# Causal attention: the mask moves from products on TensorE into a VectorE instruction that also takes the maximum

## What is computed

```
qkv = einsum('bse,ehd->bshd', x, qkv_w) + qkv_b
logits = einsum('bqhd,bkhd->bhqk', q, k) / sqrt(64)
logits = where(tril, logits, -0.7 * finfo.max)
probs = softmax(logits, axis=-1)
attn = einsum('bhqk,bkhd->bqhd', probs, v)
return einsum('bqhd,hde->bqe', attn, out_w) + out_b
```

## Time and profile before

| | us |
|---|---|
| median of 3 runs | 1450.72 |
| the profiled execution, its own time | 1447.09 |
| the profiled execution, its span | 1445.4 |
| PE busy in the span | 1402.4 (97%) |
| DVE busy | 1244.4 (86%) |
| ACT busy | 930.1 (64%) |
| POOL busy | 968.8 (67%) |

### The profile page before, as it was taken

One profiled execution on the slowest core, in us unless ns is written; L12 is line 12 of the kernel. 1 busy time (PEld: TensorE's weight loads), 2 busy tenths in 40 slices (PEclk: granted clock), 3 DMA queues, 4 the chain that ended last, 5 costly groups with the idle time before them and its releaser, 6 DMA issues.

```text
span 1445.4 us, 29493 instructions
## 1 busy us (share of the span) xinstructions
PE 1402.4 (97%) x10306; PEld 874.0 (60%) x10306; DVE 1244.4 (86%) x1966; ACT 930.1 (64%) x1862; POOL 968.8 (67%) x756
## 2 busy tenths in 40 slices
PE   8989999999999999999999997989999999999998
PEld 6645555555555555555555554556767676676777
DVE  7578788788887888878888787689999999999997
ACT  3367677766776667767677675657665576657552
POOL 5145555556555556555656554659999999999895
PEclk9999999999999999999999999999999999999999
DMA  8058777868778778787877867300000000000000
GB/s 194 1 120 208 188 172 186 198 163 193 182 175 198 167 188 194 175 193 166 194 187 180 191 163 200 91 0 1 1 8 8 1 8 1 8 9 1 8 1 15
DMA packets 77149, 164.13 MB, mean 114 GB/s; under 512 B 31410, under 2 KB 43724, under 8 KB 77004
## 3 DMA queue, kind: packets, MB, share of 16 engines
q1 hardware_dynamic: 77004, 162.24, 47.1%
HBM read 9.08 MB, written 2.10 MB: 8 GB/s over the span
## 4 chain that ended last, share of the span: by engine, by line
PE 81%; DVE 9%; issue 5%; POOL 3%; ACT 2%; DVEq 0%; POOLq 0%; ACTq 0%
PE accum L1111 17%; PE both L1045 13%; PE both L2805 8%; PE flips_all L1045 6%; PE flips_all L1137 4%; PE flips_all L2828 4%; PE misc L1009 4%; PE flips_all L1009 4%; PE flips_all L2817 3%; PE flips_all L2865 2%; PE flips_all L1022 2%; PE misc L1022 2%; PE accum L2817 2%; PE accum L2828 1%; PE flips_all L2851 1%
## 5 line engine op out<-in xcount | busy, mean ns | idle before, releaser
L462 POOL TENSOR_SCALAR big<-big,recip 128x384 f32<-128x384 f32 (+7 forms) x512 | 374.5, 746 | 401.1 <-DVE recip L714 400.8
L722 DVE STREAM_TRANSPOSE big<-big 128x896 f32<-128x896 f32 (+7 forms) x288 | 345.7, 1223 | 20.1 <-POOL big L462 19.4
L1111 PE MATMUL accum<-across,v_sb 128*64 128x256 f32 (+1 forms) x2560 | 281.9, 363 | 12.6 <-issue 12.5
L543 ACT ACTIVATE big<-both,neg_max 128x1024 f32<-128x1024 f32 (+3 forms) x256 | 242.2, 949 | 45.6 <-DVE neg_max L704 29.8
L704 DVE TENSOR_REDUCE neg_max<-both 128x1 f32<-128x1024 f32 (+3 forms) x256 | 248.5, 1011 | 24.5 <-PE both L1050 21.9
L1111 PEld LDWEIGHTS accum<-across,v_sb 128*64 128x64 f32 x2560 | 178.3, 137 | 138.7 <-issue 71.7
L1045 PE MATMUL both<-qk_sb 64*128 64x512 f32 (+3 forms) x1024 | 213.5, 535 | 10.5 <-ACT big L543 9.8
L543 ACT ACTIVATE big<-flips_all,neg_max 128x256 f32<-128x256 f32 (+3 forms) x256 | 132.0, 524 | 106.2 <-DVE neg_max L704 81.3
L1613 POOL TENSOR_TENSOR prod<-xnT,qs 128x1024 f32<-128x1024 f32 (+3 forms) x32 | 180.3, 5642 | 8.9 <-DVE qs L2318 8.9
L704 DVE TENSOR_REDUCE neg_max<-flips_all 128x2 f32<-128x512 f32 (+3 forms) x128 | 102.2, 819 | 93.8 <-PE flips_all L1050 93.1
L2805 PE MATMUL both<-slow_sb,h_T 128*128 128x512 f32 x384 | 179.7, 594 | 1.3 <-DVE xnT L2318 1.3
(11 more groups left out here) (230 smaller groups left out, 2416.2 us busy)
## 6 DMA issues: line engine op xcount, KB each, us to landing
across<-big SPq DMA_DIRECT2D x1024, 144.0 KB, 2.5
out<-x SPq DMA_DIRECT2D x8, 256.0 KB, 2.3
x<-in_L_attn_x SPq DMA_DIRECT2D x3, 512.0 KB, 5.6
slow_sb<-in_L_attn_w_slow SPq DMA_DIRECT2D x3, 512.0 KB, 7.5
w_qk<-in_L_attn_qkv_w SPq DMA_DIRECT2D x2, 512.0 KB, 6.3
xn<-in_L_ffn_W SPq DMA_DIRECT2D x1, 1024.0 KB
x<-in_L_attn_x SPq DMA_DIRECT2D x2, 256.0 KB, 3.1
qs<-in_L_attn_qkv_w SPq DMA_DIRECT2D x1, 512.0 KB, 6.3
```

Source lines behind the costliest of these rows:

```text
L462: pool.tensor_scalar(part, part, recip[:, u % 2, SLOTS.index(row), h:h + 1], 0.0, ALU.mult, ALU.add).then_inc(scaled, 1)
L543: last = act.activation(probs_of(row, h).rearrange("p b j k -> p j b k"), scores_of(row, h).rearrange("p (j b k) -> p j b k", b=MOVES, k=3 ...
L722: dve.transpose(part, part).then_inc(turned[group_of(row)], 1)
L1111: last = pe.matmul(dst, lhsT=values_of(u, j, h), rhs=keys_of(g, rows[n:n + 2], j, h), start=j == 0, stop=j == rows[n + 1])
```

## The change

The four mask products of a row are gone, and so is the building of their two operands. GpSimd now makes one bf16 tile `mask` of 128 x 1024: zeros, and the large negative number above the diagonal in its last 128 columns. For a row r the slice of its last 128 (r + 1) columns is the mask of that row. `maximum` now calls `tensor_tensor_reduce` once for each head of each row. It computes -(score + mask), writes this back to the same place in PSUM, and takes the minimum over it, which is the negated maximum of the masked scores. ScalarE's exp now reads the negated scores and has scale -1.

```diff
-        ident_half = sb("ident_half", [P, 2, P], BF16)
-        mask_half = sb("mask_half", [P, P], BF16)
+        mask = sb("mask", [P, ROWS * P], BF16)
...
-        spare = sb("spare", [P, 1008])
+        spare = sb("spare", [P, 688])
...
-            pool.memset(mask_half[:], 0.0).then_inc(const_step, 1)
-            pool.memset(ident_half[:], 0.0).then_inc(const_step, 1)
-            pool.wait_ge(const_step, 4)
-            for h in range(2):
...
-            pool.wait_ge(halves_made, 6)
+            pool.memset(mask[:], 0.0).then_inc(const_step, 1)
+            pool.wait_ge(const_step, 3)
+            own = mask[:, P * (ROWS - 1):]
+            pool.affine_select(out=own, in_=own, compare_op=ALU.is_ge, fill=MASKED, base=0,
+                               pattern=[[-1, P]], channel_multiplier=1).then_inc(mask_made, 1)
...
-                                      scores_of(row, h).rearrange("p (j b k) -> p j b k", b=MOVES, k=32), ACT.Exp,
+                                      scores_of(row, h).rearrange("p (j b k) -> p j b k", b=MOVES, k=32), ACT.Exp, scale=-1.0,
...
+                if u == 0:
+                    dve.wait_ge(mask_made, 1)
                 maxima_at.meet(u, row, *h)
                 step = step_of(row)
                 scored(u, step, h or range(2))
-                src, dst = both_scores(row), neg_max[:, u % 2, row, :]
-                if h:
-                    src, dst = scores_of(row, *h), dst[:, h[0]:h[0] + 1]
-                dve.tensor_reduce(out=dst, in_=src, axis=AX.X, op=ALU.max, negate=True).then_inc(max_ready, 1)
+                for k in h or range(2):
+                    src = scores_of(row, k)
+                    last = dve.tensor_tensor_reduce(out=src, in0=src, in1=mask[:, P * (ROWS - 1 - row):], scale=-1.0, scalar=-MASKED,
+                                                    op0=ALU.add, op1=ALU.min, accum_out=neg_max[:, u % 2, row, k:k + 1])
+                last.then_inc(max_ready, 1)
...
-                                  start=True, stop=z < hi)
-                for half in range(2):
-                    for h in range(2):
-                        part = slice(D * h, D * (h + 1))
-                        last[h] = pe.matmul(scores_of(row, h)[:, P * row + D * half:P * (row + 1)], lhsT=ident_half[part, half, :],
-                                            rhs=mask_half[part, 0:P - D * half], start=False, stop=half == 1)
+                                  start=True, stop=True)
                 return last
```

More of the change, by code:

```diff
@@ L256, in layer0 @@
         qk_loaded, v_loaded, outw_loaded = sem("qk_loaded"), sem("v_loaded"), sem("outw_loaded")
-        ident_made, const_step, halves_made = sem("ident_made"), sem("const_step"), sem("halves_made")
+        ident_made, const_step, mask_made = sem("ident_made"), sem("const_step"), sem("mask_made")
         ints_scaled, setup_flipped, bq_scaled = sem("ints_scaled"), sem("setup_flipped"), sem("bq_scaled")
@@ L388, in _ @@
             pool.memset(minus_half[:], -0.5).then_inc(const_step, 1)
-            pool.memset(mask_half[:], 0.0).then_inc(const_step, 1)
-            pool.memset(ident_half[:], 0.0).then_inc(const_step, 1)
-            pool.wait_ge(const_step, 4)
-            for h in range(2):
-                part = slice(D * h, D * (h + 1))
-                if h:
-                    pool.wait_ge(halves_made, 3)
-                pool.affine_select(out=mask_half[part, :], in_=mask_half[part, :], compare_op=ALU.is_ge, fill=MASKED, base=0,
-                                   pattern=[[-1, P]], channel_multiplier=1).then_inc(halves_made, 1)
-                for half in range(2):
-                    pool.affine_select(out=ident_half[part, half, :], in_=ident_half[part, half, :], compare_op=ALU.not_equal,
-                                       fill=1.0, base=D * half, pattern=[[-1, P]], channel_multiplier=1).then_inc(halves_made, 1)
-            pool.wait_ge(halves_made, 6)
+            pool.memset(mask[:], 0.0).then_inc(const_step, 1)
[3 more added lines that the diff above has]
+                               pattern=[[-1, P]], channel_multiplier=1).then_inc(mask_made, 1)
             def first_deviation(f):
@@ L1208, in _ @@
             pe.wait_ge(outw_loaded, 16)
-            pe.wait_ge(halves_made, 6)
             for u in range(UNITS):
```

## The result

The changed kernel takes 1454.99 us, the median of 13 runs from 1450.97 to 1458.68; before, in the same comparison, it was 1450.72. The ratio is 1.0026, with a 95% interval from 1.0015 to 1.0037. That is a real loss of 2 to 5 us, at the edge of what a measurement of this kernel can tell. The forecast was 1463, so the change was forecast at +12 us and measured at +4.3, +3.8 by the ratio.

What follows compares the result with a forecast made beforehand. The prediction took a loop from group 0's landing through VectorE and the DMA back as the bound: 25.90 + 0.44 = 26.34 us against 25.95, +12 us over 31 periods, 1459 profiled, plus 3.6 for the median: 1463 us, range 1447 to 1489.

Steps and rivals of the forecast that it cites:

- What bounds the kernel: Per unit: a loop beside TensorE's own 25.62 us stream sets the period, so relief on TensorE would not show.
- the loop: Group 0 lands, `weigh`, scores of rows 1 and 0, VectorE's maxima to row 6's transposes, DMA move: 25.90 us a unit.
- TensorE in the loop: Mask products dropped from the scores of rows 1 and 0 shorten the loop: -0.17 us.
- The elements: VectorE's new instruction runs at the reduce's pace, 1.04 ns an element.
- half pace: Rival: reading and writing the same PSUM bank makes VectorE take 2.08 ns an element and become the bound, 1676 us; chance 0.05.
- Fixed part and readout: Each new VectorE instruction costs 0.075 us fixed plus 0.07 for reading the accumulator, the latter set beside a reciprocal.
- the free readout: Rival: reading out VectorE's accumulator costs 0, the loop grows by 0.0 to 0.1 us, 1449 to 1452; chance 0.13.
- ScalarE passes the delay on: Later maxima of rows 1 and 0 delay ScalarE's work through row 6, moving row 6's reciprocal by +0.22 us.
- The sum: Row 6's transposes end 0.44 us later, so the loop becomes 26.34 us and the period grows by 0.39 us.
- The move: DMA of group 0 until it lands for `weigh`: stays at 13 us even when it starts later.
- TensorE's gain of 0.72 us: Dropping eight rows' mask products a unit only adds idle time ahead of `weigh`; TensorE's idle goes from 0.33 to about 1.4 us.
- VectorE's wait ahead of step 4: VectorE's idle time before the maxima of rows 1 and 0, whose scores are step 4, shrinks from 2.6 to about 1.9 us.

Runs made afterwards that it cites:

- Experiments 3 and 4: Kernel before with the new masking only in rows 3 to 7, or only in rows 0 to 2: ratios 0.9985 and 1.0037.
- experiment 10: Kernel before with one reduce for each head in rows 0 to 3, no new mask or readout: 1454.54 against 1450.04 us, ratio 1.003.
- experiments 7 and 8: Scores of rows 0 and 1 moved ahead of `weigh` on TensorE, in the changed kernel and the one before: 1442.87 and 1447.26 us.
- Experiments 5 and 6: Row 2's maximum moved behind row 6's transposes, ScalarE and TensorE reordered, in the changed kernel and the one before: 1472.85 and 1462.50 us.
- experiment 2: Kernel before, mask products kept, with the new VectorE instruction adding a mask of zeros: 1468.63 against 1452.21 us, ratio 1.0109.

## Why the prediction was right in sign and three times too large

**What bounds the kernel** held in its main point. TensorE has 0.66 us less to do in a unit, and the kernel got slower. Experiments 3 and 4 put the cost on the three small rows, experiment 10 shows that a fifth of a microsecond there costs what the whole change costs, and with the maxima of rows 1 and 0 off the way from the landing, in experiments 7 and 8, the sign turns. But the loop is not alone. Within the 29 periods `weigh` waited in 17 units after the change and in 14 before, about half. Experiments 5 and 6 ran into a second loop at once, and the chain of the changed kernel goes along it. The prediction knew only the first loop. The change lengthens a stretch that both share, so this did not cost it the sign, which is in part luck. One unit's sum that comes to the whole period does not prove that no other path comes to it as well.

**TensorE in the loop**: forecast -0.17 us, measured -0.21 (2.98 to 2.77). Right.

**The elements**: forecast 1.04 ns each, measured 1.05. Right; the rival of half pace is out.

**Fixed part and readout** is the step that was mis-sized: "0.80 + 4 (0.075 + 0.07) = 1.38" was measured as 1.23, and "0.80 + 2 (0.075 + 0.07) = 1.09" as 1.00. In place of 0.145 us for each main instruction with its readout it is 0.10 to 0.11. The bound from below, the free readout, was nearer than the reciprocal that I chose, which is an instruction with work of its own. Of the +0.43 us in the loop, 0.21 are the splitting (experiment 10) and 0.22 the rest. The Trainium skill's fixed 120 cycles (0.125 us) for PSUM in "VectorE: DVE Perf Modes", the section on the TRN2 errata, is not what these steps show: 0.07 for the reduce, 0.10 to 0.11 with the readout. Its section on DRAIN says that the next op does not start until the pipe is empty, and that one which is not held starts earlier. Here one starts at 627.50 while the one ahead is reported until 627.58; the rows do not show when its pipe was empty.

**ScalarE passes the delay on**: right. The exp of rows 1 and 0 started 1.05 us behind the maxima before and 1.40 after (628.17, in ScalarE's timeline below), and the reciprocal of row 6 came 6.19 us behind them before and 6.52 after.

```profile
628.17 0.47 ACT L534 ACTIVATE big<-flips_all,neg_max 128x256 f32<-128x256 f32 x1 [1.30 <-DVE neg_max L696]
```

**The sum.** The loop grew by 0.33 - 0.21 + 0.13 = 0.25 us in place of 0.44. From the 25.90 us that I put for the loop this makes 26.15, and the period is 26.13: +0.18 us, over 31 periods 5.6 us. The same sum with the measured price would have said 26.15 - 25.95 = 0.20 us a unit, 6 us, 1457. The medians are 4.3 us apart, the ratio says 3.8. So the price makes up 6 of the 8 us that the forecast was too high. The remaining 2 us are less than what the two profiled executions differ by beyond the medians (2.8 us), so no cause can be named for them. That sum and period agree to 0.02 us is partly chance, since 25.90 was an estimate and half the units do not wait for the landing.

**The move** stayed at 13 us, so it gave next to nothing back. Right: in the units in which `weigh` waited it took 13.25 us on average before and 13.18 after. In experiment 7's chain most of such a move is the issuing of the 16 transfers.

**One term of a rival** does not follow from its own parts: in "21.9 + 1.7 + 9.6" the 1.7 us should be 16 x 0.145 - 12 x 0.07 = 1.5. Nothing hangs on it, since half pace did not come.

**Two marks were wrong.** "TensorE's gain of 0.72 us becomes idle time ahead of `weigh`": its idle time did rise to 1.17 us a unit (forecast 1.4), but the rise is ahead of scores and projections that wait for exps (9.8 to 22.5 us for `both`), not ahead of `weigh` (12.5 to 12.8). And VectorE's wait ahead of step 4 was to shrink from 2.6 to 1.9 us; it is 2.60 in the unit shown and 72.0/32 = 2.25 on average, where it was 82.4/32 = 2.58. So it shrank by half of what I said.

**What stays open**: how experiment 2's 15.8 us divide between the landing and the new wait ahead of the projections, and how the change's 3.8 us divide between the two loops. Experiment 5 shows what the second loop can do, and the chain that the changed kernel runs along it, but no run takes one loop away and leaves the other as it was.

## What to carry to other kernels

An engine at 97% need not be the bound, and one at 86% can be: read the period from one landing to the next and see on which instructions the loop steps, then price an edit there alone. When two loops are nearly as long as the engine's own stream, moving work from one loop to the other makes it worse; cutting the tie between them, here by one line that lets scores go ahead of the products that wait for a DMA, was worth more than the change. And short instructions are counted by number: splitting a few of them cost as much as the whole exchange.

## What the runs showed of the hardware

An instruction with an accumulator readout is listed as two rows on VectorE, the second of 139 ns. It does not hold the engine for that time: the next main instruction starts at the same instant as the readout (627.12 in the rows above), and six such instructions together cost 0.22 us more than six plain reduces.

The 16 transfers of a group follow one another in SyncE's queue, in the chain of experiment 7 mostly 0.63 us apart. So of a group's move of 13 us the issuing is 10.3 us, and the way of the last transfer 2.5 us.

The granted clock of TensorE fell in the start of the profiled execution of the changed kernel, in two stretches where it was full before. Windows 23 to 28 and 74 to 79 us, after:

```profile
23.00:28.00 5.00, 5.00 (x20) 2.87 (x19) 4.62 (x22) 2.25 (x4) 1.19 (x3) 0.66 1.28 221
74.00:79.00 5.00, 4.19 (x16) 2.20 (x17) 0.87 (x2) 2.86 (x11) 2.23 (x2) 0.66 0.00 0
```

And before:

```profile
23.00:28.00 5.00, 4.89 (x28) 3.56 (x29) 4.79 (x21) 3.30 (x5) 1.42 (x2) 1.00 1.24 223
74.00:79.00 5.00, 5.00 (x38) 3.89 (x40) 2.37 (x4) 3.08 (x11) 2.23 (x2) 1.00 0.00 2
```

The clock is the column ahead of the DMA's share: 0.66 on average, so a good part of each stretch ran at the lower level of 1.2 GHz. Ahead of the first, TensorE had been idle for 1.48 and 0.47 us, almost the same as before the change (1.49 and 0.48), where the clock stayed full. In the second, TensorE had been idle for 2.69 us, and the eight products behind that took 3.34 us; before, the same products took 1.77 us behind 2.44 us of idle time. First the row after the change, then the one before it:

```profile
74.81 3.34 PE L1039 MATMUL both<-qk_sb 64*128 64x512 f32 x8 [2.69 <-ACT big L534]
```

```profile
73.93 1.77 PE L1045 MATMUL both<-qk_sb 64*128 64x512 f32 x8 [2.44 <-ACT big L543]
```

These stretches lie ahead of the second unit's transpose, and these eight slower products alone are 1.6 of the 2.5 us by which it comes later. Other experiments show such a lapse in one, both or neither of the stretches, with and without the new mask, so I do not put it down to the change. It says that two single profiles can differ by 2 or 3 us for a reason that lies outside of what was changed.
